# Expert layer in windows of 32 tokens with four column tiles, in place of windows of 128 tokens with split weights

## The reference, cut to what matters

```python
x_flat = x.reshape(b * t, d)                       # 512 tokens of 512
logits = x_flat @ w_gate + b_gate                  # 8 experts
route_p = jnp.max(softmax(logits), axis=-1); route_idx = jnp.argmax(...)
h = relu(jnp.einsum('nd,edm->enm', x_flat, W1) + b1[:, None, :])    # 512 -> 2048
y = jnp.einsum('enm,emd->end', h, W2) + b2[:, None, :]              # 2048 -> 512
out = y[route_idx, jnp.arange(n)] * route_p[:, None]
```

## Time and profile before

| | before |
|---|---|
| median of three runs | 414.92 us (414.63 to 416.57) |
| profiled execution, first to last instruction (span) | 413.7 us |
| expert windows, first product to last | 176.4 to 405.7 us |
| PE busy | 383.1 us, 93% of the span |
| DVE busy | 325.5 us, 79% |
| ACT busy | 262.1 us, 63% |
| POOL busy | 61.2 us, 15% |
| DMA moved | 97.61 MB |

### The profile page before, as it was taken

How to read it: one execution, slowest core, us unless ns; L and a number is a source line. 1 busy time by engine, 2 the same in 40 slices (tenths; PEclk the granted TensorE clock), 3 DMA queues, 4 the chain that set the end, 5 groups by cost and what they waited for, 6 DMA issues and landing times.

```text
span 413.7 us, 5739 instructions
## 1 busy us (share of the span) xinstructions
PE 383.1 (93%) x1642; PEld 274.0 (66%) x1642; DVE 325.5 (79%) x512; ACT 262.1 (63%) x397; POOL 61.2 (15%) x63
## 2 busy tenths in 40 slices
PE   0999999999997997699999899999999999999992
PEld 0766576578974466477677676777767678676770
DVE  1788968897574786669898698898988989898870
ACT  4879988772220121468686686867778687796840
POOL 2230000000000010300130301204022040400402
PEclk9999999999999996989999999999999999999997
DMA  8999881695539700420068999889999999940100
GB/s 178 390 345 387 306 315 78 255 352 206 204 114 401 296 2 6 105 76 0 0 228 305 370 412 387 304 303 371 343 373 401 337 390 344 370 140 1 41 0 1
DMA packets 36046, 97.61 MB, mean 236 GB/s; under 512 B 3049, under 2 KB 5737, under 8 KB 34482
## 3 DMA queue, kind: packets, MB, share of 16 engines
q1 hardware_dynamic: 31954, 90.57, 59.6%
q0 software_dynamic: 2432, 6.60, 5.2%
q10 hardware_dynamic: 1632, 0.11, 0.4%
HBM read 94.09 MB, written 3.68 MB: 236 GB/s over the span
## 4 chain that ended last, share of the span: by engine, by line
PE 90%; DMA 2%; DVE 2%; issue 2%; ACT 2%; POOL 1%; SPq 0%; ACTq 0%; POOLq 0%; DVEq 0%
PE bank L1552 51%; PE bank L1376 7%; PE bank L1357 7%; PE bank L1568 4%; PE bank L1386 3%; DMA ring<-in_wq_t 2%; PE bank L1309 2%; PE bank L1337 2%; PE bank L1422 2%; PE bank L1365 1%; PE bank L1429 1%; PE bank L1302 1%; PE bank L1400 1%; PE bank L1344 1%; ACT w_hi L720 1%
## 5 line engine op out<-in xcount | busy, mean ns | idle before, releaser
L1194 DVE TENSOR_TENSOR w_lo<-ring,w_hi 128x1024 fp32r<-128x1024 f32 x117 | 144.7, 1264 | 27.0 <-ACT w_hi L720 24.2
L720 ACT ACTIVATE w_hi<-ring 128x1024 fp32r<-128x1024 f32 x117 | 122.1, 1053 | 49.1 <-PE bank L1552 48.1
L1552 PE MATMUL bank<-w_hi,x_hi 128*128 128x512 f32 x144 | 49.9, 428 | 4.1 <-ACT w_hi L720 4.1
L1552 PE MATMUL bank<-ring,work 128*128 128x512 f32 x108 | 49.3, 592 | 0.0
L1552 PE MATMUL bank<-w_hi,x_lo 128*128 128x512 f32 x144 | 45.8, 399 | 1.2 <-issue 1.2
L1552 PE MATMUL bank<-w_lo,x_hi 128*128 128x512 f32 x144 | 45.7, 398 | 0.0
L1552 PEld LDWEIGHTS bank<-w_hi,x_hi 128*128 128x128 f32 x144 | 26.8, 192 | 13.3 <-ACT w_hi L720 6.5
L1282 POOL TENSOR_TENSOR small<-small,x_ext 128x512 f32<-128x512 f32 x9 | 15.0, 1664 | 130.9 <-ACT small L728 130.9
L1552 PE MATMUL bank<-w_hi,h_hi 128*128 128x512 f32 x90 | 33.3, 451 | 0.0
L1552 PEld LDWEIGHTS bank<-w_hi,x_lo 128*128 128x128 f32 x144 | 27.3, 190 | 8.1 <-issue 1.7
L1552 PEld LDWEIGHTS bank<-ring,work 128*128 128x128 f32 x108 | 19.8, 190 | 18.0 <-issue 17.2
(11 more groups left out here) (192 smaller groups left out, 600.9 us busy)
## 6 DMA issues: line engine op xcount, KB each, us to landing
ring<-in_w SPq DMA_DIRECT2D x32, 2048.0 KB, 10.7
ring<-in_ctx_turned SPq DMA_DIRECT2D x4, 2048.0 KB, 12.0
ring<-in_ctx SPq DMA_DIRECT2D x4, 2048.0 KB, 13.2
x_ext<-sorted_rows POOLq DMA_DIRECT2D x9, 257.0 KB, 3.0
work<-in_b SPq DMA_DIRECT2D x8, 256.0 KB, 7.8
ring<-in_wq_t SPq DMA_DIRECT2D x4, 256.0 KB, 9.3
x_ext<-in_x SPq DMA_DIRECT2D x4, 256.0 KB, 9.4
x_ext<-in_bv POOLq DMA_DIRECT2D x4, 256.0 KB, 12.2
```

The costliest lines, as they stand in the source:

```text
L720: act.activation(w_hi[:, n % NSPLIT, :, :], weight_part(e, n), ACT.Identity).then_inc(hi_ready, 1)
L1194: dve.tensor_tensor(w_lo[:, n % NSPLIT, :, :], weight_part(e, n), w_hi[:, n % NSPLIT, :, :], ALU.subtract).then_inc(lo_ready, 1)
L1552: ins = pe.matmul(dst, kept, moved, start=start and g == 0 and q == 0, stop=stop and g == 1 and q == len(terms) - 1)
```

## The change

A window is 32 tokens (`WIN`), so the kept operand of a product is 32 columns wide and its output fills 32 PSUM partitions. Four such products stand one after the other in the program, each with its own weights columns and its own 32 PSUM partitions (`t * WIN`). All products of the expert layer are plain fp32; the splits of weights, tokens and hidden values are gone, from ACT and DVE alike.

First product (`hidden`, twice per window): for each of 4 blocks of the contraction, 4 products of 256 weight columns, one per partition group; 32 products a window. DVE turns the result in blocks of 32 by 32 (`hidden_turned`, 128 by 256 at once), adds the bias (`bias_added`), ACT applies ReLU (`hidden_relu`). Second product (`output`, twice): 8 blocks of hidden values, block j to partition group j mod 4, 512 columns each; 16 products a window. The four partition groups then hold four partial sums, and DVE adds them one after the other onto the residual row (`output_added` three times, then `output_done` into `y_out`). This is done inside the next window's pass; one extra pass stands at the end. PE waits for `y_read` before it writes the output bank again, and `output_done` waits until the scatter of the window before has landed (`rows_sent`), since there is one `y_out`.

The ring has ten places: the two that held the split weights join it. They hold sorting data until the tokens are sorted, so eight units are loaded early as before (`EARLY`) and two more right after the sorting.

```diff
-MAXW = NE + (NB * LQ - NE) // P
-NSLOT = 8
+WIN = 32
+NT = P // WIN
+MAXW = NE + (NB * LQ - NE) // WIN
+NSLOT = 10
+EARLY = 8
...
-            return (0, 2, 1, 3, 4, 5, 7, 6)[j % NSLOT]
+            return (0, 2, 1, 3, 4, 5, 7, 6, 8, 9)[j % NSLOT]
...
+        def hidden_weights(e, g, d, t):
+            place = ring[:, weight_place(UNITS * e + g), :].rearrange("p (d j q) -> p d j q", d=DCH, j=JCH)
+            return place[:, d, :, t * WIN:(t + 1) * WIN]
+        def output_weights(e, g, j):
+            return ring[:, weight_place(UNITS * e + 2 + g), :].rearrange("p (j n) -> p j n", j=JCH)[:, j, :]
...
-            for j in range(NSLOT, NE * UNITS):
-                sp.wait_ge(parts_used, PARTS * last[e] + 2 * block + 2)
+            for j in range(EARLY, NE * UNITS):
+                if j >= NSLOT:
+                    e, u = divmod(j - NSLOT, UNITS)
...
+                    sp.wait_ge(units_used, UNITS * last[e] + u + 1)
...
-                act.activation(w_hi[:, n % NSPLIT, :, :], weight_part(e, n), ACT.Identity).then_inc(hi_ready, 1)
...
+            def window_copied(w, row):
+                act.wait_ge(units_used, UNITS * w + 2)
+                act.activation(x_win, xs_t[:, :, bass.ds(row, WIN)], ACT.Identity).then_inc(x_win_ready, 1)
+            def hidden_relu(w, g):
+                act.wait_ge(h_added[g], w + 1)
+                act.activation(h_t[g], h_sum[g], ACT.Relu).then_inc(h_ready[g], 1)
...
-                dve.tensor_tensor(w_lo[:, n % NSPLIT, :, :], weight_part(e, n), w_hi[:, n % NSPLIT, :, :],
-                                  ALU.subtract).then_inc(lo_ready, 1)
...
+            def output_added(w, t):
+                if t > 0:
+                    dve.wait_ge(parts_added, (NT - 1) * w + t)
+                dve.scalar_tensor_tensor(out=y_sum[:, 0:D], in0=output_part(t), scalar=y_weight,
+                                         in1=y_sum[:, 0:D], op0=ALU.mult, op1=ALU.add).then_inc(parts_added, 1)
+            def output_done(w):
+                dve.wait_ge(parts_added, (NT - 1) * (w + 1))
+                dve.wait_ge(rows_sent, 16 * w + 32)
+                dve.scalar_tensor_tensor(out=y_out[:, 0:D], in0=output_part(NT - 1), scalar=y_weight,
+                                         in1=y_sum[:, 0:D], op0=ALU.mult, op1=ALU.add).then_inc(y_read, 1)
+                dve.tensor_copy(y_out[:, D + 1:D + 2], y_sum[:, D + 1:D + 2]).then_inc(y_ready, 1)
+            def hidden_turned(w, g):
+                dve.wait_ge(units_used, UNITS * (w + 1) + g + 1)
+                dve.transpose(h_raw[g].rearrange("p j s -> p (j s)"), bank[:, H_BANK[g], 0:GN]) \
+                    .then_inc(h_turned[g], 1)
+            def bias_added(e, w, g):
+                dve.wait_ge(h_turned[g], w + 2)
...
+                dve.tensor_tensor(h_sum[g], h_raw[g], bias, ALU.add).then_inc(h_added[g], 1)
...
+                        dve.wait_ge(units_used, UNITS * w + UNITS)
+                        dve.wait_ge(y_sum_ready, w + 1)
+                        output_added(w, 0)
+                        output_added(w, 1)
+                        hidden_turned(w, 0)
+                        bias_added(e, w, 0)
+                        output_added(w, 2)
+                        output_done(w)
+                        hidden_turned(w, 1)
+                        bias_added(e, w, 1)
+                        next_rows(e, w)
...
+            def send_rows(w):
+                pool.wait_ge(y_ready, w + 1)
...
+                pool.indirect_dma_start(out, bass.IndirectOffsetOnAxis(ap=y_out[:, D + 1:D + 2].bitcast(U32), axis=0),
...
+                        pool.dma_start(x_rows_w, sorted_rows[bass.ds(first_row, WIN), :]).then_inc(x_rows_loaded, 16)
+                        send_rows(w)
...
+            def hidden(e, w, g):
...
+                pe.wait_ge(x_win_ready, w + 1)
+                pe.wait_ge(h_turned[g], w + 1)
+                for d in range(DCH):
+                    for t in range(NT):
+                        dst = bank[t * WIN:(t + 1) * WIN, H_BANK[g], 0:GN].rearrange("s (j q) -> s j q", j=JCH)
+                        ins = pe.matmul(dst, x_win[:, d, :], hidden_weights(e, g, d, t), start=d == 0, stop=d == DCH - 1)
+                ins.then_inc(units_used, 1)
+            def output(e, w, g):
...
+                pe.wait_ge(h_ready[g], w + 1)
+                if g == 0:
+                    pe.wait_ge(y_read, w + 1)
+                for j in range(JCH):
+                    t = j % NT
+                    ins = pe.matmul(bank[t * WIN:(t + 1) * WIN, Y_BANK, :], h_t[g][:, j, :], output_weights(e, g, j),
+                                    start=g == 0 and j < NT, stop=g == 1 and j >= JCH - NT)
+                ins.then_inc(units_used, 1)
...
                         hidden(e, w, 0)
                         hidden(e, w, 1)
-                        turn_hidden(w, 0)
...
                         output(e, w, 0)
-                        hidden(e, w, 3)
...
                         output(e, w, 1)
```

More of the change, by code:

```diff
@@ L73 @@
 T0, T1, T2, O_BANK = 4, 5, 6, 7
-H_BANK, T_BANK, Y_BANK = (4, 5), (6, 7), 0
+H_BANK, Y_BANK = (4, 5), T2
 FILLS = [(S_BANK[d], ("wqk", d)) for d in range(DCH)]
@@ L376, in window_row @@
         def window_row(offset, i):
-            return nc.s_assert_within(offset + i * P, 0, NB * P,
+            return nc.s_assert_within(offset + i * WIN, 0, NB * P,
                                       skip_runtime_bounds_check_because="windows cover only the tokens there are")
[L380 to L418, removed]
+        def hidden_weights(e, g, d, t):
[3 more added lines that the diff above has]
+            return ring[:, weight_place(UNITS * e + 2 + g), :].rearrange("p (j n) -> p j n", j=JCH)[:, j, :]
         block = stack.enter_context(nc.Block())
@@ L722, in outputs_copy @@
[L722 to L732, removed]
@@ L734, in block_relu @@
-            def block_relu(e, w, k):
-                block_may_relu(act, 0, w, k)
-                for i in range(HB_CH):
-                    m = 2 * HB_CH * k + i
-                    ins = act.activation(hid[0][:, i * P:(i + 1) * P], bank[:, T_BANK[0], i * P:(i + 1) * P], ACT.Relu,
-                                         bias=b1_sb[:, e, m:m + 1])
-                ins.then_inc(h_relu[0], 1)
-            def block_high(w, i):
-                p, k = i % 2, i // 2
-                act.wait_ge(h_relu[p], 2 * w + k + 2)
-                wait_block(act, w, "o", i - 2 if p == 0 else i - 4)
-                act.activation(h_hi[:, p, :, :], hid[p].rearrange("p (m s) -> p m s", m=HB_CH), ACT.Identity) \
-                    .then_inc(h_hi_ready[p], 1)
@@ L752, in _ @@
+            for c in range(DCH):
+                after_read(act, ("xs", c))
+            act.wait_ge(pad_ready, 1)
             for e in range(NE):
@@ L1530, in _ @@
                     sorting(c, batches)
-            def products(e, w, what, i, dst, rows, start, stop, low_rows, high_rows):
-                for g in range(2):
-                    n = 2 * BLOCKS.index((what, i)) + g
-                    if n in WHOLE:
-                        unit = unit_of(e, n)
-                        pe.wait_ge(place_loaded[weight_place(unit)], 16 * weight_count(unit))
-                        terms = [(hid[i % 2][:, col_slice(2 * g + c)], weight_part(e, n)[:, c, :]) for c in range(2)]
-                    else:
-                        high_rows()
-                        pe.wait_ge(hi_ready, HALVED * w + halved(n))
-                        terms = [(rows(x, 2 * g + c), part[:, n % NSPLIT, c, :])
-                                 for x, part in ((0, w_hi), (1, w_hi), (0, w_lo)) for c in range(2)]
-                    for q, (kept, moved) in enumerate(terms):
-                        if n not in WHOLE and q == 2:
-                            low_rows()
-                        if n not in WHOLE and q == 4:
-                            pe.wait_ge(lo_ready, HALVED * w + halved(n))
-                        ins = pe.matmul(dst, kept, moved,
-                                        start=start and g == 0 and q == 0, stop=stop and g == 1 and q == len(terms) - 1)
-                    ins.then_inc(parts_used, 1)
@@ L1571, in output @@
[L1571 to L1577 removed]
+            def hidden(e, w, g):
+                unit = UNITS * e + g
+                pe.wait_ge(place_loaded[weight_place(unit)], 16 * weight_count(unit))
+                pe.wait_ge(x_win_ready, w + 1)
[5 more added lines that the diff above has]
+                ins.then_inc(units_used, 1)
```

214 lines of the change are left out of this document (61 added, 153 removed).

## The result

The changed kernel takes **390.19 us** (median of 4 runs, 386.4 to 394.07), the kernel before in the same measurement 415.75 (median of 4, 414.63 to 417.02). The ratio is 0.937, with a 95% interval of 0.930 to 0.944; it leaves out the changed kernel's slowest run, 394.07, which is on record as a slow one. The forecast was 364.5. The time lies inside the range on record, but 6 us outside the forecast's own range of 348 to 384, so a term of the sum was missing or too small.

The account below looks back on a forecast made before the run. PE bounds the kernel, DMA next: first window at 176.4 us, eleven windows 94.6, first unit and gap to 274.9, 14 weight units to 350.4, landing and tail to 363.3, plus 1.2: 364.5 us; own range 348 to 384, recorded 347 to 452.

Parts of the forecast that it names:

- the range on record: Whole kernel: 347 to 452 us, stretched to reach the case of two passes at a time.
- the two-pass rival: PE's products: a product's two passes queue, so two overlap, not four; 13.8 us a window, 450 us; chance 0.32.
- the output ring: Single output row buffer: the fourth add waits for the previous scatter; 385 to 420 us, chance 0.08.
- four tiles side by side: PE's window products: four partition groups overlap, 8.6 us a window instead of 27.6; 348 to 384 us, chance 0.54.
- The cycle: Time from one 32-token window to the next in the expert loop: 8.6 us, between 7.6 and 10.3.
- The open price: PE's time per pass with four products side by side, seen in no trace row: 0.080 us first product, 0.107 second.
- weights at the end: From the twelfth window on DMA sets the end: 14 weight units of 5.4 us, 75.5 us, against 8.6 us windows.
- unit 18: First of the last 14 weight units, forecast to start loading at 274.9 us, in the twelfth window.
- the step from the fifth window to the twelfth: Expert 2's windows: its second-layer weights are wanted about when they land, so only 1.25 us is added.
- the gap: The 1.25 us "issue" gap of the old trace, added once for expert 2's second-layer weights.
- The tail after PE: After the last products: four adds and hand-over 3.1 us, then POOL and the scatter 5.8 us.
- Strict order of the passes: PE starts matmuls strictly in program order, so two overlap: 13.8 us a window, 450 us; chance 0.32.

Follow-up runs that it names:

- run 5: Run 1's kernel, with ACT instead of DVE taking the fourth partial sum out of PSUM; 363.23 us, ratio 0.875 to the kernel before.
- run 1: The changed kernel with four places for the `b2` rows instead of two, so they load experts ahead; 372.92 us, ratio 0.899 to the kernel before.
- run 4: Run 1's kernel with only an eighth of each weight unit loaded from the eleventh unit on; 347.89 us, measured once.
- run 2: The changed kernel, still two `b2` places, with ACT issuing the `b2` rows from its own queue; 374.12 us, ratio 0.902 to the kernel before.
- run 3: The changed kernel with products reordered, eight first-product or four second-product passes of one column tile in a row; 425.14 us, measured once.
- run 7: Run 1's kernel with the first tile's eight first-product passes ahead of the other three tiles', which take turns; 380.76 us, measured once.

## Why the prediction was right, and where it was wrong

That the range on record holds 390.19 is owed to its width, which was taken for the two-pass rival; between 385 and 420 the prediction had expected only the output ring, at 0.08, and the ring is not what happened.

**Right: four tiles side by side.** The cycle is 8.14 us where 8.6 was forecast, inside 7.6 to 10.3. The open price came out as 0.055 us a pass in the first product (0.080 taken, 0.054 the lower bound) and 0.114 in the second (0.107 taken). Because the first product is faster than assumed, PE waits about 1.05 us per window for the fourth add, as the prediction said it would at 0.054; run 5 takes this wait away and gains 0.96 us a window. So 8.14 is near 8.6 partly by luck: about 3.5 us of first product where 5.1 were taken, and a wait that the forecast did not have. Of the two rows behind DVE's price for an add out of PSUM, the one of 0.744 us reads `work` and not PSUM; the adds out of PSUM took 0.742 to 0.751, so nothing hangs on it.

**Right: weights at the end.** PE's waits for `ring` in the changed kernel, 13.2 us, fall after unit 18 but for 1.45, while DMA moves 386 to 406 GB/s; its last windows, though, end on a `b2` row. Once `b2` is out of the way, the last product waits for the last unit (run 1), and an eighth of the bytes gives back 25 us (run 4).

**Wrong: the step from the fifth window to the twelfth, "so I add 1.25 us there".** The sum took weights and DVE's windows as all that counts between the fifth window and unit 18, and never counted the `b2` rows in SP's queue, though the loop that loads the weights issues them too, once per expert, behind four units. Unit 18 left at 288.90 and not 274.9, 14.0 late, and this is how that adds up:

- the first window ends at 190.2 and not at 185.0: +5.2. DVE's first add waits for the scatter of the sorted rows, which lands 7.14 us after 172.46, and the second product, after 4.63 us of waiting, is slower, 5.34 us for 3.64. The prediction named this wait but gave it no price;
- four windows of expert 0, 33.0 for 34.4: -1.4;
- the next two, 190.2 + 33.0 = 223.2 to 254.55, 31.35 for 18.45 (two windows and the gap): **+12.9**. Run 1 takes 19.2 for them, so 12.2 are the `b2` row;
- four windows of 8.14, 32.6 for 34.4, and a first unit of 1.76 for 2.6: -2.6.

From unit 18 to PE's end it took 90.2 us and not 79.5: +10.7. Run 1 splits this. 3.9 are `b2` again; 4.8 are the 14 units, whose last lands about 354.69 - 272.07 = 82.6 us after the first was issued and not 77.8, 5.9 us a unit with its landing for the 5.4 of an unbroken stretch; about 1.9 is the last product at half clock, 3.64 for 1.7. The tail after PE was 10.9 for 8.9: +2.0. Together 363.3 + 14.0 + 10.7 + 2.0 = 390.0, the span. So the `b2` rows explain about 16.1 of the 26.7 us that were missing (12.2 + 3.9). Runs 1 and 2, which remove them in two different ways, gain 17.3 and 16.1 us of the median; of span they gain 20.9 and 19.4, of which 4.6 and 3.1 lie in the first two windows.

**The rivals.** Strict order of the passes (13.8 us a window, 450 us) did not come: adjacent passes of one product do not hold up the next tile. The Trainium skill's rule that matmuls start and end in program order (TensorE: Matmul & The Clock Gate, "Part 3: Packing small matmuls — row/col tiling"), read as the prediction reads it, disagrees with this trace: 32 passes in 1.76 us. Runs 3 and 7 show that something of the kind exists all the same, only later: with eight passes of a tile in a row the products fall to two at a time, with two or four in a row they do not. The Trainium skill's gain of 2.38 times for three column tiles, in the same section, from which I estimated 3.2 times for four, is less than the 3.9 and 3.8 measured. The output row ring did not come either: in 20 fourth adds DVE waited 0.2 us for a scatter, though the chain passes once through one (6.48 us from 300.55).

## What to carry to other kernels

When a change makes an engine four times as fast, list every load that stands in the same DMA queue as the big ones, also the small ones, and ask when each is now wanted: loads of 64 KB behind 8.4 MB took up to 19.62 us to land, and moving them to another queue or loading them earlier gave back 16 to 17 us of the median. Small tiles in an fp32 matmul paid fully when the program went round the tiles every one or two products; with four products of a tile in a row the first product ran two tiles at a time, not four (run 3). And price a wait twice where PE stands still long enough for its granted clock to fall: once for the wait, once for the slower products behind it.

## What the runs showed of the hardware that was not expected

- Four 32-column fp32 tiles reach 3.8 to 3.9 times the rate of one after the other, weight loads included: 0.055 us per 256-column pass against 0.216.
- A column tile seems to hold four passes, the running one among them; the next one stops the passes behind it in the program. Two, four and eight passes in a row (the changed kernel, and both products of run 3) and the four lone starts of run 7 agree with it. Runs of five to seven passes were not tried, and whether the limit belongs to the tile or to how far PE looks ahead in all stays open. It counts passes and not columns, as four of 512 columns in a row (run 3) held up nothing, as many columns as eight of 256.
- After a wait of 3.21 us PE's granted clock was 0.50, and the same 16 passes took 3.64 us for 1.92 (run 1).
- A load of 64 KB behind 8.4 MB of weights in one queue took 19.62 us from issue to landing; on another queue, with the weights moving as before, 5.0 to 6.3 (run 2).
